# Two expert blocks in every fourth step to the end of the loop, and the sixteen zero fills moved to the first slots of the drain

## The chip, the cores and the metric

The kernel runs on one core of one Trainium2 chip. The metric is the time of one execution of the whole program on the device, in microseconds (us); less is better. Besides TensorE (PE), VectorE (DVE), ScalarE (ACT) and GpSimd (POOL), the sync engine (SP) matters here: it computes nothing, and issues most of the transfers, one after the other.

## What is computed

The reference takes 6250 rows of 256 numbers and 100,000 edges sorted by target. It normalizes the rows, and adds to each row a graph convolution and a linear attention. Then each normalized row z is sent to its two best of 16 experts:

```python
gate_logits = x @ gate_w + gate_b
topk_vals, topk_idx = jax.lax.top_k(gate_logits, K)          # K = 2 of E = 16
topk_w = jax.nn.softmax(topk_vals, axis=-1)
h = jax.nn.relu(jnp.einsum('bsh,ehf->bsef', x, w1) + b1)
expert_out = jnp.einsum('bsef,efh->bseh', h, w2) + b2
moe = jnp.sum(topk_w[..., None] * sel, axis=2)               # sel: the two chosen experts' rows
y = x + moe                                                  # then a last normalization of y
```

The output is the sum of the stages, 6250 x 256.

## The kernel before, in words

Rows are handled in 49 tiles (t) of 128, edges in 782 chunks (c) of 128. After a preparation of some 240 us comes **the loop** of 101 steps, a table that `plan` works out when the program is built. Step g (0 to 97) handles 8 chunks of edges: POOL issues 8 indirect gathers into a ring of 24 places in SBUF (`gather`, L1108), DVE makes one-hot matrices (L1585, L1590), PE adds the chunks up in PSUM with two `quad`s of 4 chunks (L2069). In between the tiles that are complete go through graph layer, attention, gate and sorting: `E`, `A`, `B`, `Q1`, `Q2` of a step are the tiles whose parts it does. After a tile's B, DVE has the slot of each row with each of its experts, and three steps later POOL scatters the rows to the DRAM tensor `disp`, ordered by expert (`dispatch`, L1116).

**A block** (in the code an item, k from 0 to 117) is 128 rows of one expert. SP loads it transposed from `disp` into one of four buffers (`item_rows`, `flip_rows`, L620), when the block four before it has left its buffer. PE multiplies by the first weights (`item_one`, L2168 and L2171: 28 matmuls), ACT takes the positive part (L1312), DVE makes the low half of the hidden rows (`hidden_lo`, L1814), PE multiplies by the second weights (`item_two`, L2182 and L2187: 13 matmuls), ACT evicts (L1319) and stores to the DRAM tensor `ytok` (L1306). Which expert and which rows make a block is decided on the device, two blocks at a time, by `pick_pair` on DVE (L1766 to L1787), out of the rows that `dispatch` has placed; blocks 58 to 73 are a fixed round over all experts (`flush`), and so are the last sixteen, 102 to 117. `room` says how many blocks `plan` may put into a step: two where the step's number is in `DOUBLE` and the step has no E and no B, else one. The second block of a step stands on PE behind the step's second quad, and its `item_two` in the next step behind that step's first quad.

**The drain** is what follows the loop: the blocks that found no step (`TAILK`), one in each slot j. PE does `item_one` of the next block and then `item_two` of this one, in two pairs of PSUM banks. In the same slots runs the last stage for tiles 0 to 31, in pieces of two tiles. POOL gathers each row's two expert outputs (`final_pool`, L814), DVE sums and measures (`final_sum`, L823 to L835) and normalizes (`final_norm`, L843 to L854), and SP stores both tiles and loads `zpd` and `zd` for tiles six later (`f_store` and `f_load`, L795, L789, L790). There are 8 buffers of tiles. `early` spreads the 32 pieces of work (`EARLY`: 16 sums, 16 norms) evenly over the slots, from two steps ahead of slot 0 on. **After the drain** the tiles 32 to 48 are done in the same way. Their gathers wait until all blocks are stored.

The last sixteen blocks read 128 rows of each expert that may lie partly behind the last row placed. So each expert's 128 rows behind its end are set to zero first: `fill_ends` (L983 to L988), 16 DMAs of 128 KB issued by SP, each with the register of its place loaded ahead. `item_rows` of the blocks from 102 on waits until all have landed. The places (`endoff`) are written by DVE in `ends`, behind the last pick. `left` is the semaphore by which DVE tells that such tables are written.

The part of `plan` that takes a block's step from `room`:

```python
while last < len(steps) and len(steps[last].item) >= room(steps[last], last):
    last += 1
at[k] = last
if last < len(steps):
    steps[last].item.append(k)
```

Of the kernel before, what the change touches and what calls it, by code (L numbers as in the profile page):

```python
# [10 lines left out]
P = 128  # L11
# [7 lines left out]
EXP = 16  # L19
CAP = 6528  # L20
# [7 lines left out]
ND = KB + 2 * JB  # L28
# [51 lines left out]
A_STEP = 16  # L80
NH = 4
NEARLY = 8
DOUBLE = range(32, 81, 4)


def static(k):
# [18 lines left out]
def room(s, i):  # L105

    return 2 if i in DOUBLE and not s.E and s.B is None else 1

# [99 lines left out]
class Own:  # L208
# [5 lines left out]
    def then(self, ins):  # L214
        self.n += 1
        ins.then_inc(self.on.sems[self.name], 1)
        return self.n
# [5 lines left out]
def build(nc, A, out):  # L223
# [11 lines left out]
    def sb(name, shape, dt):  # L235
        return ctx.enter_context(nc.sbuf_tensor(name, shape, dt))

    def dram(name, shape, dt):
        return nc.dram_tensor(name, shape, dt, kind="Internal").ap()
# [6 lines left out]
    S = Sems()  # L246
# [56 lines left out]
    tailt = sb("tailt", [P, EXP], f32)  # L303
# [21 lines left out]
    endoff = sb("endoff", [1, EXP], i32)  # L325
# [51 lines left out]
    disp = dram("disp", [DROWS, 2 * ROW], f16)  # L377
# [228 lines left out]
    redo = [misc[:, tok0 + 256 * i:tok0 + 256 * i + 256] for i in range(4)]  # L606

    def settled(e):
        e.wait_ge(S["left"], 3)
        f = e.value_load(flag[0:1, 2:3], min_val=0, max_val=1)  # L610
        return f

# [9 lines left out]
    def spare_sp(e):  # L622
        f = settled(e)
        st = rawslot[:, 13, :]
        with e.If(f):
            spare_idle(e)
            for i in range(SPARE):
                e.wait_ge(S["spare_dve"], i * SDV + 9)
                x = e.value_load(imax[0:1, 0, 0:1], min_val=0, max_val=EXP - 1)
                a_ = e.value_load(ioff[0:1, 0, 0:1], min_val=0, max_val=EXP * CAP - P)  # L630
                flip_rows(e, a_, 0)
                e.wait_ge(S["iz0"], 16 * (len(range(0, NI, 4)) + i + 1))
                for h, n in enumerate(("w1p", "w2p")):
                    e.dma_start(st[:, h * 1024:h * 1024 + 1024],
                                A[n][bass.ds(x, 1), :, :].rearrange("a p c -> (a p) c")).then_inc(S["spare_sp"], 16)
                e.wait_ge(S["spare_act"], i * SAC + SAC)
                e.dma_start(ytok[bass.ds(a_, P), :], iy[0].bitcast(i32)).then_inc(S["spare_sp"], 16)
                e.wait_ge(S["spare_sp"], i * SLD + SLD)
            for u in range(FB):
                e.wait_ge(S[f"sto{u}"], stored(FE, u))  # L640
            for t in range(FE):
                e.dma_start(redo[2], zpd[t * P:t * P + P, :]).then_inc(S["spare_sp"], 16)
                e.dma_start(redo[3], zd[t * P:t * P + P, :]).then_inc(S["spare_sp"], 16)
                e.wait_ge(S["spare_dve"], SPARE * SDV + RDV * (t + 1))
                e.dma_start(out[t * P:t * P + P, :], redo[3]).then_inc(S["spare_sp"], 16)
                e.wait_ge(S["spare_sp"], SPARE * SLD + RLD * (t + 1))

    def spare_dve(e):
        f = settled(e)
        sm, st = isml[:, 0, :], rawslot[:, 13, :]  # L650
        h = ih[0]
# [215 lines left out]
    with ctx:  # L867
# [3 lines left out]
        def _(e):  # L871
# [90 lines left out]
            def item_rows(k):  # L962
                if k >= 4:
                    on.wait_ge("il1", k - 3)
                if KF <= k < KB:
                    dispatched(FLT)
                    on.wait_ge("left", 1)
                    e.reg_load([yreg], flushoff[0:1, k - KF:k - KF + 1])
                elif k < ND:
                    j = pair_of(k)  # L970
                    dispatched(SEEN[j])
                    on.wait_ge("wlo", 4 * EXP)
                    on.wait_ge("pick", j + 1)
                    e.reg_load([yreg], ioff[0:1, j % 4, k % 2:k % 2 + 1])
                else:
                    dispatched(NT - 1)
                    on.wait_ge("fill", 16 * (2 + EXP))
                    e.reg_load([yreg], tailoff[0:1, k - ND:k - ND + 1])
                flip_rows(e, e.snap(yreg, min_val=0, max_val=DROWS - P), k % 4)

            freg = e.alloc_register(name="fill")

            def fill_ends():  # L983
                on.wait_ge("left", 2)
                for x in range(EXP):
                    e.reg_load([freg], endoff[0:1, x:x + 1])  # L986
                    e.dma_start(disp[bass.ds(e.snap(freg, min_val=0, max_val=EXP * CAP - P), P), :],  # L987
                                A["zrows"][0:P, :]).then_inc(S["fill"], 16)  # L988

            def final_stores(j):  # L990
                for c, p in early(j):
                    if c == "norm":
                        for t in PIECES[p]:
                            f_store(e, on, t)
# [43 lines left out]
            for j, k in enumerate(TAILK):  # L1038
                while loaded < min(k + 5, NI):
                    item_rows(loaded)  # L1040
                    loaded += 1
                if k == ND - 5:
                    fill_ends()
                final_stores(j - 1)
            final_stores(len(TAILK) - 1)
            spare_sp(e)
# [94 lines left out]
        def _(e):  # L1141
# [186 lines left out]
            def weights(n):  # L1328
                x = WORDER[n]
                for u in range(4):  # L1330
                    on.wait_ge(f"ld_wt{u // 2}", 16 * (n + 1))
                    if n >= 14:
                        on.wait_ge("wlo", 4 * n)
                    elif n >= 7:
                        on.wait_ge("ctxs", min(NT, (2048 * (x + 1) - 1) // 258 + 1))
                    hi_o, _, raw = wparts(x, wstage(n), u)
                    e.activation(hi_o, raw, ACT.Copy, scale=16.0).then_inc(S["whi"], 1)
# [65 lines left out]
        def _(e):  # L1403
            on = Waits(e, S)
            own = Own(on, "own_dve")
            then = own.then
# [342 lines left out]
            hold = {}  # L1749
# [58 lines left out]
            def hidden_lo(k, j):  # L1808
                j = max(j, 0)
                bank_ = (H[:, :], agg[:, 512:1024])[j % 2]  # L1810
                on.wait_ge("irelu", k + 1)
                on.wait_ge("il2", k if j == 0 else k - 1)
                h = ih[j % 2]
                e.scalar_tensor_tensor(h[:, 512:1024], bank_, 0.0, h[:, 0:512], ALU.max, ALU.subtract).then_inc(S["ilo"], 1)  # L1814
# [13 lines left out]
            def finals(j):  # L1828
                for c, p in early(j):
                    (final_sum if c == "sum" else final_norm)(e, on, own, p)  # L1830
# [55 lines left out]
            def ends():  # L1886
                own.wait_ge(hold["head"])
                own.wait_ge(own.n)
                then(e.tensor_copy(endoff[:, :], tailt[0:1, :]))
                f_ = then(e.tensor_scalar(fullb[:, :], tailt[:, :], 128.0, None, ALU.subtract))  # L1890
                x = then(e.tensor_tensor(isml[:, 3, 0:16], tailt[:, :], head[:, :], ALU.subtract))
                own.wait_ge(x)
                x = then(e.tensor_reduce(join[0:1, 1:2], isml[0:1, 3, 0:16], AX.X, ALU.max))
                own.wait_ge(f_)
                e.tensor_tensor(tailoff[:, :], fullb[0:1, :], snap[0:1, :], ALU.max).then_inc(S["left"], 1)
                own.wait_ge(x)
                x = then(e.tensor_scalar(join[0:1, 1:2], join[0:1, 1:2], 128.0, None, ALU.is_gt))
                own.wait_ge(x)
                x = then(e.tensor_tensor(join[0:1, 1:2], join[0:1, 1:2], join[0:1, 2:3], ALU.max))
                own.wait_ge(x)  # L1900
                e.tensor_copy(flag[0:1, 2:3], join[0:1, 1:2]).then_inc(S["left"], 1)

            def late_picks(slot_):
                for j, t in LATE:
                    if late_at(j) == slot_:
                        pick_pair(j, t)
                        if j == JF - 1:
                            flush()
                        if j == JF + JB - 1:
                            ends()  # L1910

            on.wait_ge("seen", NT)
            for j, k in enumerate(TAILK):
                if j == 0:
                    late_picks(0)
                    hidden_lo(k, 0)
                if j + 1 < len(TAILK):
                    hidden_lo(TAILK[j + 1], j + 1)
                finals(j)
                if j:  # L1920
                    late_picks(j)
# [413 lines left out]
```

## Time and profile before

| | |
|---|---|
| median of 3 runs | 1520.53 us (1517.84 to 1522.57) |
| profiled execution | 1516.08 us, of which the span of the trace 1514.2 us |
| PE busy | 1137.3 us (75%) |
| DVE busy | 1030.5 us (68%) |
| POOL busy | 1040.8 us (69%) |
| ACT busy | 452.7 us (30%) |
| the loop's last gather is issued at | 1268.49 us |
| the drain's first block starts on PE at | 1313.41 us |
| the drain's last block starts its last group on PE at | 1449.99 us |

The span runs from the first to the last instruction of the trace; 1.9 us of the execution lie around it. An engine's busy time leaves out register loads, branches and the issuing of DMAs; "issue" in a row is time in which an engine waited for nothing that the profile shows. SP's queue is written SPq, and the time of a row there is what the instruction held SP, not what the transfer took. PE is pipelined, so that the ends of its rows overlap the next one's start; starts are the better measure.

### The profile page before, as it was taken

The page shows a single profiled execution, that of the slowest core. Times are in us where ns is not written, and L with a number is a line of the kernel's source. Part 1 is how long each engine was busy: PE and PEld are TensorE (multiplying, and loading weights), DVE is VectorE, ACT ScalarE, POOL GpSimd, SP SyncE. Part 2 cuts the span into 40 slices and gives each one's busy share as a digit, 9 for nine tenths or more (in the row PEclk, how much of TensorE's full clock was granted, in tenths as well). Part 3 has the DMA queues.
Part 4 walks back from the last instruction along what each step waited for, and adds up shares of the span by engine and source line. Part 5 has one row for each costly group of instructions (what it writes and reads, how often), then busy time and mean ns, then how long its engine had stood idle before and what let it go on. Part 6 is the DMA issues. An engine that isn't in the chain of part 4 may idle for free. (4 is left out here: it accounts for less than half of the span.)

```text
span 1514.2 us, 34216 instructions
## 1 busy us (share of the span) xinstructions
PE 1137.3 (75%) x10594; PEld 986.1 (65%) x10594; DVE 1030.5 (68%) x3731; ACT 452.7 (30%) x1286; POOL 1040.8 (69%) x1068
## 2 busy tenths in 40 slices
PE   2338999667768988888888987887978878596930
PEld 2327788556557877777777876776867767575820
DVE  7863666577787767676675767665666566694767
ACT  3763455222222322222222222232222223221310
POOL 3657777767757777777777777777777776442535
PEclk9999999887778999999998999999989899798975
DMA  8238777544456666556555555566555555587965
GB/s 258 75 101 268 243 252 251 183 129 141 155 156 162 162 160 160 160 149 167 159 155 157 154 161 158 148 170 164 147 154 155 149 151 151 145 207 189 251 182 168
DMA packets 214482, 257.79 MB, mean 170 GB/s; under 512 B 92690, under 2 KB 177382, under 8 KB 213994
## 3 DMA queue, kind: packets, MB, share of 16 engines
q0 software_dynamic: 47328, 128.21, 31.0%
q1 hardware_dynamic: 149978, 111.76, 25.6%
q10 hardware_dynamic: 16992, 15.47, 3.3%
q8 instruction: 102, 1.67, 0.5%
q14 instruction: 82, 0.67, 0.2%
HBM read 179.45 MB, written 64.86 MB: 161 GB/s over the span
## 5 line engine op out<-in xcount | busy, mean ns | idle before, releaser
L1108 POOL DMA_INDIRECT ring<-ytab,src x782 | 778.1, 995 | 259.3 <-issue 234.1
L2069 PE MATMUL agg<-ring,oh 128*128 128x256 f16 x2346 | 313.5, 287 | 104.4 <-DMA ring<-ytab,src 104.4
L2069 PEld LDWEIGHTS agg<-ring,oh 128*128 128x128 f16 x2346 | 260.5, 117 | 137.1 <-issue 117.8
L2171 PE MATMUL H<-misc,big 128*128 128x128 f16 x2448 | 203.6, 229 | 0.3
L2171 PEld LDWEIGHTS H<-misc,big 128*128 (+1 forms) x2448 | 172.1, 102 | 15.9 <-issue 2.0
L2187 PE MATMUL OB<-big,misc 128*128 (+1 forms) x1224 | 156.2, 279 | 0.0
L814 POOL DMA_INDIRECT ring<-ytok,slot x74 | 73.3, 991 | 92.5 <-DMA out<-ring 50.6
L1116 POOL DMA_INDIRECT disp<-misc,slot x98 | 103.8, 1059 | 47.6 <-issue 45.4
L2187 PEld LDWEIGHTS OB<-big,misc 128*128 128x128 f16 x1224 | 119.5, 100 | 16.9 <-issue 0.2
L1590 DVE TENSOR_TENSOR oh<-eq,whl 128x1024 f16<-128x1024 f16 x196 | 127.1, 690 | 3.4
L1814 DVE SCALAR_TENSOR_TENSOR misc<-H,misc 128x512 f16<-128x512 f32 x102 | 70.3, 689 | 59.3 <-ACT misc L1312 57.8
L2168 PE MATMUL H<-sel,bank 80*128 (+1 forms) x408 | 94.2, 231 | 9.7 <-issue 6.6
L1312 ACT ACTIVATE misc<-H 128x512 f16<-128x512 f32 x102 | 60.5, 593 | 104.1 <-PE H L2171 89.0
L1319 ACT ACTIVATE misc<-OB 128x256 f32<-128x256 f32 x102 | 39.1, 383 | 156.9 <-PE OB L2187 156.5
L1259 ACT ACTIVATE small<-small,eps 128x1 f32<-128x1 f32 x98 | 28.8, 294 | 163.6 <-DVE small L1639 157.9
L1266 ACT ACTIVATE misc<-QT 128x256 f32<-128x256 f32 x49 | 18.8, 385 | 162.5 <-PE QT L2095 162.5
L1585 DVE TENSOR_TENSOR eq<-iota,loc 128x1024 f16<-128x1024 f16 x98 | 65.9, 672 | 0.0
L1612 DVE SCALAR_TENSOR_TENSOR misc<-misc 128x256 f32<-128x256 f32 x49 | 20.9, 429 | 63.3 <-ACT misc L1231 63.3
L2116 PE MATMUL QT<-wpj,misc 128*128 128x256 f32 x196 | 59.0, 429 | 0.0
L1283 ACT ACTIVATE misc<-GB 128x256 f32<-128x256 f32 x49 | 18.6, 379 | 134.9 <-PE GB L2123 132.9
L2095 PE MATMUL QT<-misc,wq 128*128 128x128 f32 x392 | 54.5, 283 | 5.0 <-DVE misc L1685 4.7
L2123 PE MATMUL GB<-ident,misc 128*128 128x128 f32 x98 | 23.3, 325 | 45.4 <-DVE misc L1696 45.4
(282 smaller groups left out, 2365.9 us busy)
## 6 DMA issues: line engine op xcount, KB each, us to landing
ytok<-misc ACTq DMA_DIRECT2D x118, 128.0 KB
ring<-ytab,src POOLq DMA_INDIRECT x782
big<-in_w1p SPq DMA_DIRECT2D x15, 512.0 KB, 4.2
big<-in_w2p SPq DMA_DIRECT2D x15, 512.0 KB, 6.3
big<-in_x_pt SPq DMA_DIRECT2D x7, 896.0 KB, 12.1
ytab<-big SPq DMA_DIRECT2D x7, 896.0 KB, 4.1
selfr<-ytab SPq DMA_DIRECT2D x49, 128.0 KB
xtd<-misc SPq DMA_DIRECT2D x49, 128.0 KB, 6.0
```

What stands on the lines that cost most here:

```text
L814: e.indirect_dma_start(v[0:n, j, :].bitcast(i32), None, ytok, bass.IndirectOffsetOnAxis(ap=slot[0:n, t, j:j + 1], axis=0)).then_inc(S[f"in ...
L1108: e.indirect_dma_start(ring[:, (c % R) * 512:(c % R) * 512 + 512], None, ytab[0:NP, :], bass.IndirectOffsetOnAxis(ap=src[:, c:c + 1], axis ...
L1116: e.indirect_dma_start(disp, bass.IndirectOffsetOnAxis(ap=slot[:, t, j:j + 1], axis=0), zhl[t % 2], None).then_inc(S[f"sc{j}_{t % 2}"], 16)
L1312: e.activation(ih[max(j, 0) % 2][:, 0:512], bank_, ACT.Relu).then_inc(S["irelu"], 1)
L1585: return then(e.tensor_tensor(eq[:, :, :, :], iota_p, spots(loc[:, :], g), ALU.is_equal))
L1590: e.tensor_tensor(oh[:, g % 2, j], eq[:, :, :, :], spots(whl[:, j, :], g), ALU.mult).then_inc(S["oh"], 1)
L1814: e.scalar_tensor_tensor(h[:, 512:1024], bank_, 0.0, h[:, 0:512], ALU.max, ALU.subtract).then_inc(S["ilo"], 1)
L2069: m_ = e.matmul(o_, oh[:, g % 2, wp, (c % 8) // 4, :, c % 4], ring[:, a_ + 256 * yp:a_ + 256 * yp + 256], start=False, stop=True, skip_gro ...
L2116: m_ = e.matmul(QT[:, 256:512], eb[:, o_ * 128:o_ * 128 + 128], wpj[:, o_, :], start=False, stop=o_ == 1)
L2168: e.matmul(o_, bank[:, f * 128:f * 128 + 128], who, start=True, stop=False)
L2171: m_ = e.matmul(o_, ws(h * 1024 + wp * 512 + f * 128, 128), zp[:, h * 128:h * 128 + 128], start=False, stop=(h == 1 and q == 2))
L2187: m_ = e.matmul(O, hp[:, f * 128:f * 128 + 128], w_, start=False, stop=(f == 3 and q == 2))
```

## The change

`DOUBLE` reaches to step 98 instead of 80. The fills are issued in four groups of four, in the drain's slots 1, 3, 5 and 7, instead of all sixteen in slot 12, where block 97 was; each group has one load of four registers. The places are written at the start of the drain, which adds one to the counts of `left`.

```diff
-DOUBLE = range(32, 81, 4)
+DOUBLE = range(32, 99, 4)
...
     def settled(e):
-        e.wait_ge(S["left"], 3)
+        e.wait_ge(S["left"], 4)
...
-            freg = e.alloc_register(name="fill")
-
-            def fill_ends():
+            fregs = [e.alloc_register(name=f"fill{i}") for i in range(4)]
+
+            def fill_ends(q):
                 on.wait_ge("left", 2)
-                for x in range(EXP):
-                    e.reg_load([freg], endoff[0:1, x:x + 1])
-                    e.dma_start(disp[bass.ds(e.snap(freg, min_val=0, max_val=EXP * CAP - P), P), :],
+                e.reg_load(fregs, endoff[0:1, 4 * q:4 * q + 4])
+                for r in fregs:
+                    e.dma_start(disp[bass.ds(e.snap(r, min_val=0, max_val=EXP * CAP - P), P), :],
                                 A["zrows"][0:P, :]).then_inc(S["fill"], 16)
...
-                if k == ND - 5:
-                    fill_ends()
+                if j % 2 and j // 2 < 4:
+                    fill_ends(j // 2)
...
             def ends():
                 own.wait_ge(hold["head"])
                 own.wait_ge(own.n)
-                then(e.tensor_copy(endoff[:, :], tailt[0:1, :]))
...
             on.wait_ge("seen", NT)
+            own.wait_ge(hold["tail"])
+            e.tensor_copy(endoff[:, :], tailt[0:1, :]).then_inc(S["left"], 1)
             for j, k in enumerate(TAILK):
```

Worked out by `plan`, the steps 84, 88, 92 and 96 now have two blocks. The drain has 29 blocks (89 to 117) instead of 33 (85 to 117). Two picks that were made in the drain are made in the loop, which leaves three of the five, and the 32 pieces of the last stage lie closer.

DVE, the end of step 84. L1666 is the last of the step's attention sum, L1766 and L1768 begin the pick:

```order
 L1639 BN_AGGR small<-small 128x2
 L1666 SCALAR_TENSOR_TENSOR misc<-misc 128x256
+L1814 SCALAR_TENSOR_TENSOR misc<-H,misc 128x512
 L1766 TENSOR_TENSOR isml<-seen_tail,head 128x16
 L1768 MAX isml<-isml 128x8
```

The step's second block adds its low half there; the same stands at the end of steps 88, 92 and 96.

SP before, in slot 12, behind the load of block 101. The three rows of a fill stand sixteen times:

```order
L974 TENSOR_LOAD ioff [waits k_pick,k_il1]
L979 ISA
L620 DMA_TRANSPOSE misc<-disp 128x4x128
...
L620 DMA_TRANSPOSE misc<-disp 128x4x128
L986 TENSOR_LOAD endoff [waits k_left]
L987 ISA
L987 DMA disp<-in_zrows 16x4096
L986 TENSOR_LOAD endoff
...
L978 TENSOR_LOAD tailoff [waits k_fill,k_il1]
L979 ISA
L620 DMA_TRANSPOSE misc<-disp 128x4x128
```

SP now, in slot 3, between the load of block 96 and that of block 97:

```order
L620 DMA_TRANSPOSE misc<-disp 128x4x128
L985 TENSOR_LOAD endoff
L987 ISA
L987 DMA disp<-in_zrows 16x4096
L987 ISA
L987 DMA disp<-in_zrows 16x4096
L987 ISA
L987 DMA disp<-in_zrows 16x4096
L987 ISA
L987 DMA disp<-in_zrows 16x4096
L974 TENSOR_LOAD ioff [waits k_il1]
```

Between two loads of blocks stand four fills and one register load, where sixteen fills and sixteen register loads stood.

## Rows read from the trace of the kernel before

**Rows 1.** Windows of stages: stretch, us, busy per engine (count), clock, DMA share, GB/s

```profile
0.00:1270.00 1270.00, 990.18 (x8993) 861.75 (x8994) 862.39 (x3129) 399.31 (x1136) 935.91 (x963) 0.92 0.58 167
...
1310.00:1452.00 142.00, 121.11 (x1370) 102.20 (x1370) 105.18 (x372) 38.77 (x101) 53.23 (x55) 0.93 0.84 208
1452.00:1514.20 62.20, 0.00 (x0) 0.00 (x0) 40.16 (x129) 4.50 (x18) 34.50 (x34) 0.53 0.55 165
...
1390.00:1450.00 60.00, 53.14 (x658) 49.03 (x659) 44.41 (x128) 18.22 (x48) 23.63 (x24) 0.91 0.96 237
```

**Rows 2.** Windows of two stretches of the loop, columns as above

```profile
500.00:600.00 100.00, 86.59 (x837) 75.78 (x837) 71.93 (x286) 26.90 (x81) 76.64 (x77) 0.97 0.65 167
1100.00:1200.00 100.00, 76.11 (x698) 68.08 (x696) 62.38 (x230) 23.54 (x72) 76.56 (x77) 0.90 0.58 155
```

**Rows 3.** Waits of POOL, 500 to 1100 us: us in total, times, longest

```profile
POOL ring L1108 <- PE agg L2069: 0.6, 2, 0.3
```

**Rows 4.** The longest wait of PE, 1100 to 1270 us

```profile
PE agg L2069 <- DMA ring<-ytab,src: 35.9, 12, 5.1
```

**Rows 5.** Timeline of PE, loop's end: start, us, line; in brackets the idle before

```profile
1264.96 1.47 PE L2187 MATMUL OB<-big,misc 128*128 x12
1269.08 1.50 PE L2069 MATMUL agg<-ring,oh 128*128 128x256 f16 x12 [2.65 <-DMA ring<-ytab,src]
```

**Rows 6.** Timeline of PE, the drain

```profile
1327.47 1.48 PE L2187 MATMUL OB<-big,misc 128*128 x12
...
1374.63 1.48 PE L2187 MATMUL OB<-big,misc 128*128 x12
...
1391.09 0.29 PE L2168 MATMUL agg<-sel,bank 80*128 80x128 bf16 x1 [11.05 <-DMA misc<-disp]
...
1405.82 1.47 PE L2187 MATMUL agg<-big,misc 128*128 128x256 f16 x12
...
1411.82 1.47 PE L2187 MATMUL agg<-big,misc 128*128 128x256 f16 x12
...
1422.36 0.29 PE L2168 MATMUL agg<-sel,bank 80*128 80x128 bf16 x1 [2.83 <-DMA misc<-disp]
...
1449.99 1.48 PE L2187 MATMUL OB<-big,misc 128*128 128x256 f16 x12
```

**Rows 7.** Timeline of SP's queue, the drain

```profile
1368.77 17.20 SPq L987 DMA_DIRECT2D disp<-in_zrows  x16
1388.33 1.26 SPq L620 DMA_TRANSPOSE misc<-disp  x1
...
1401.70 3.27 SPq L620 DMA_TRANSPOSE misc<-disp  x2
...
1423.56 2.88 SPq L620 DMA_TRANSPOSE misc<-disp  x2
...
1429.96 3.51 SPq L620 DMA_TRANSPOSE misc<-disp  x2
...
1437.37 2.88 SPq L620 DMA_TRANSPOSE misc<-disp  x2
```

**Rows 8.** Two lines of SP: duration of one in ns, min/median/max

```profile
L986 SPq TENSOR_LOAD <-endoff x16: 260/266/416, 1368.3 to 1385.0; - x16
L987 SPq DMA_DIRECT2D disp<-in_zrows x16: 517/517/1396, 1368.8 to 1385.5; - x16
```

**Rows 9.** The chain of waits at PE's second stop

```profile
1416.33 5.99 DMA misc<-disp
```

**Rows 10.** Waits of PE, 800 to 930 us, all of them

```profile
PE agg L2069 <- DMA ring<-ytab,src: 8.5, 4, 3.7
PE GB L2123 <- DVE misc L1696: 4.5, 4, 1.3
PE OB L2182 <- DVE misc L1814: 2.5, 2, 1.2
PE H L2168 <- issue: 1.9, 5, 0.6
```

## The prediction

> **What bounds the kernel now.** I read the windows first, since the program has stages. The loop's gathers end near 1270 us, 40 us follow in which the last tiles pass through, the drain fills 1310 to 1452, and 62.2 us of POOL gathers and DVE work close the span [rows 1]. Then I asked in each stage which wait ends last.
>
> In the loop it is POOL. It issues 77 indirect transfers per 100 us, both in the stretch where steps with two blocks occur (500 to 600) and where they have stopped (1100 to 1200), while PE is 86.59 us busy in the first and 76.11 in the second [rows 2]. The rest of those 100 us, 23.4, is 0.3 us behind each transfer. For a place in the ring, which only PE can free, it waited 0.6 us in 600 [rows 3]. PE is the one that waits: from 1100 to 1270 it stood 35.9 us for gathered chunks [rows 4].
>
> In the drain PE is bound while it is fed. From 1327.47 to 1374.63 it does 12 blocks, 3.93 us each. The blocks with a fixed expert take 3.00 us (1405.82 to 1411.82, two blocks). In between it stands for 11.05 us, waiting for the transposed load of block 102, and once more for 2.83 us at 1422.36 [rows 6]. SP's queue shows why: sixteen fills hold it for 17.20 us from 1368.77, and the next block load leaves only at 1388.33 [rows 7].
>
> **The change, part by part.** Durations come from the profiled execution, 1516.08 us.
>
> Loop. Each of four steps gets a block more, 3.93 us of PE at the drain's price, 15.7 us together. Per four steps (36 POOL transfers at 100/77 us, 46.8 us) PE has 35.9 x 46.8 / 170 = 9.9 us of waiting for chunks. So 3.9 us fit in, and POOL's pace stays: 0 us. Without that cover the price would be 15.7 us. DVE gets one row of `hidden_lo` more in each such step and is 62.38% busy there [rows 2]; SP's transposed loads come with it, in a stretch where the DMA engines' share is 0.58 [rows 2]. Both at 0. At the very end the cover is thinner. Step 96's second block puts its second group behind step 97's first quad, where a chunk wait of 2.65 us ended at 1269.08; that group is 1.47 us long at 1264.96 [rows 5] and stood ahead of the wait before. What follows in steps 97 to 100 moves by it, with its bias matmul, by **+1.6**. Bounds: 0 (the later waits of that chain swallow it) and +3.9 (a whole block).
>
> Drain, blocks with a picked expert. Thirteen instead of 17, at 3.93 us: **-15.7**. DVE also loses two picks from it. I cost that at 0, since PE sets the pace there.
>
> Fills. The stop of 11.05 us goes: **-11.05**. It needs all sixteen landed before block 102 is loaded, and in the new order the last group is issued in slot 7, block 102's load in slot 9. What do they cost where they stand now? A register load is 0.27 us and a fill 0.52 [rows 8]. With some 0.14 us of gaps behind each fill, as in the old pitch of about 1 us, a group is 0.27 + 4 x 0.66 = 2.9 us of SP. A pair of slots on SP (two transposed loads, two stores, four loads) takes 6.40 us at the best (1423.56 to 1429.96) [rows 7]. With a group that is 9.3 against 7.86 of PE, so SP falls behind by 1.4 us in each of four pairs, 5.8 us in all. SP may run three blocks ahead, 11.8 us, less what a load needs until PE has it: 2.8 us (issued 1388.33, PE starts 1391.09) to 6.0 (the chain's 5.99) [rows 6, 7, 9]. That leaves 5.8 to 9.0, just enough. I take **+1**, with bounds of 0 and 11.6 (all four groups exposed).
>
> The DMA engines carry the 2 MB of fills earlier, beside loads and stores. The rows say that this stretch has a share of 0.84 on average [rows 1]. The Trainium skill (DMA: Bandwidth & Descriptors, section "Issuing engines are not separate DMA queues") says that DMAs run on the same 16 engines whichever engine issues them, and interleave. By it, moving or regrouping an issue saves sequencer time alone and no transfer, and where those engines are full the sum would be the first rival's, a gain of 20 to 25 us instead of 28.
>
> Drain, last sixteen blocks. Here PE was not the bound before: from 1391.09 to 1449.99 + 1.48 they took 60.4 us [rows 6], where 16 x 3.00 + 1.6 (the second group of block 101) = 49.6 would do. Once the stops are gone SP is late next. From 1401.70 to 1437.37 it made five pairs in 35.7 us, 7.13 each [rows 7], against PE's 6.0 per pair. Eight pairs make 57.0. SP now arrives with part of its lead intact, of which I count 2 us. So 57.0 - 2 + 1.6 = 56.6, a gain of **-3.8**. Bounds: -10.8 (PE's own pace) and 0 (nothing, should the lead be used up by the fills).
>
> After the drain: the 62.2 us start when the last block is stored, and do the same work. 0.
>
> Sum: 1.6 - 15.7 - 11.05 + 1 - 3.8 = **-27.95**, so 1488.1 us for a profiled execution. The median of the runs stands 4.45 above the profiled one (1520.53 against 1516.08), which gives **1492.5**.
>
> **The rivals.**
>
> *The DMA engines set the drain.* It moved 208 GB/s x 142 us = 29.5 MB at a share of 0.84 [rows 1]. Four blocks go to the loop with 128 KB in and 128 KB out each, 1.05 MB. The remaining 28.5 MB at full share (208 / 0.84 = 248 GB/s) take 115 us, and at the 237 GB/s of 1390 to 1450 [rows 1] 120. The drain's window then shrinks by 22 to 27 us, with 1.6 us at the loop's end a gain of 20.4 to 25.4, or about 1497.5. For it: the share is 0.96 over the last blocks already [rows 1]. Against: part of that is the work that the fills had held back, and my own sum puts the drain's end at 1422 to 1424, within 3 us of this case's better end.
>
> *The fills stop PE.* If SP has no lead in slots 1 to 7 (loads landing after 6 us or more), the groups are exposed with 11.6 us instead of 1, and the last blocks gain nothing: -27.95 + 10.6 + 3.8 = -13.5, or 1507. Against it stands the lead worked out above, for it that the lead is used up to within a microsecond.
>
> *Slower: the block loads reach the loop before their rows.* Picks and uses stand closer now. The pair of blocks 84 and 85 was picked in step 94 and used from step 100 on; now it is picked in 92 and used in 96 and 97. Its load leaves SP a step earlier, and waits for a scatter that POOL issues after the gathers of group 94. Behind that load wait SP's loads and stores for the tiles. Should each of the pairs 84/85, 86/87 and 88/89 cost a step of 11.7 us, 35.1 us, the change loses: 1492.5 + 35.1 = 1527.6. It decides from 28 / 3 = 9.3 us per pair. Against it: between 800 and 930 us blocks are used three steps after their pick with two blocks in every fourth step, and PE's list of waits has no transposed load in it [rows 10].
>
> *The step's table does nothing.* Not so here: the four steps have neither E nor B, and the added rows of DVE show the blocks. Only the loop's own cover could fail: if PE's waits for chunks were not slack but a clock that the gathers keep, +15.7 would eat the drain's -15.7, leaving -12.3, or 1508. The even 77 transfers speak against it.
>
> **How the numbers follow.** Forecast 0.55; DMA-bound drain 0.22; exposed fills 0.10; loop without cover 0.03; late loads 0.04, of which 0.03 end slower and 0.01 in the middle; 0.06 for a smaller loss of several kinds, two thirds of it still faster. About 0.3% (4.6 us) is what a measurement can tell from no change. Faster 0.94, same 0.03, slower 0.03. The forecast's bounds give 1520.5 - 37.5 = 1483 at the low end (no loop end, no fill cost, PE's own pace) and -11.3, or 1509, at the high end (3.9 at the loop's end, fills exposed, no gain in the last blocks). The range of 1482 to 1506 holds the forecast, the DMA case and part of the third.
>
> **What would show it.** In the changed trace: POOL still at 77 transfers per 100 us up to 1270 us and its last gather of edges within 2 us of 1268.5; PE's waits for chunks between 1100 and 1270 down from 35.9 to about 20 us; the drain's first block near 1315; no PE wait over 3 us near its middle; SP's queue with four groups of four fills of some 2.9 us; PE's last group near 1422 to 1424; some 62 us behind it. I am wrong if POOL waits for PE's ring places, if the last blocks come every 3.0 us (more gain), or if PE waits for transposed loads between slots 3 and 12 (less).

## The result, and the profile after

The changed kernel takes **1498.82 us** (median of four runs, 1496.45 to 1502.07) where the kernel before took 1520.62 beside it (four runs): a ratio of 0.9859, with a 95% interval of 0.9834 to 0.9885. The gain is 21.8 us where 28 were forecast. The profiled execution took 1496.45 us, 19.6 less than the one before, and its span is 1494.5 us.

The windows of the changed kernel (stretch, us, busy per engine with counts, granted clock, DMA share, GB/s):

```profile
0.00:1270.00 1270.00, 1005.59 (x9173) 870.86 (x9174) 868.73 (x3150) 402.08 (x1144) 927.86 (x964) 0.93 0.60 168
1310.00:1432.00 122.00, 106.04 (x1211) 91.26 (x1211) 97.17 (x335) 35.28 (x94) 53.04 (x54) 0.94 0.90 231
1432.00:1494.50 62.50, 0.00 (x0) 0.00 (x0) 39.98 (x129) 4.50 (x18) 34.81 (x34) 0.51 0.56 167
1320.00:1370.00 50.00, 45.06 (x467) 35.48 (x468) 38.12 (x135) 13.96 (x36) 19.20 (x20) 0.97 0.85 215
1370.00:1420.00 50.00, 44.11 (x564) 41.38 (x561) 41.17 (x122) 14.85 (x41) 28.31 (x29) 0.93 1.02 263
1100.00:1200.00 100.00, 83.04 (x802) 74.36 (x803) 65.95 (x248) 25.80 (x78) 76.24 (x79) 0.93 0.60 163
```

Against [rows 1], PE does 15.4 us more in the same 1270 us of loop, and the drain's window is 20 us shorter. Against [rows 2], PE rose by 7 us in 1100 to 1200 and POOL did not slow down (79 transfers against 77). The use of the loop's cover is seen in PE's longest wait from 1100 to 1270 us, which was 35.9 us for chunks [rows 4]:

```profile
PE agg L2070 <- DMA ring<-ytab,src: 17.4, 10, 3.7
```

The waits of PE in the changed drain, 1310 to 1440 us. `H`, `agg` and `OB` are PSUM tiles, `misc<-disp` is a block's transposed load, L1814 is `hidden_lo`; total, times, longest:

```profile
PE agg L2169 <- DMA misc<-disp: 4.3, 3, 2.9
PE OB L2183 <- DVE misc L1814: 3.1, 3, 1.4
PE agg L2183 <- DVE misc L1814: 3.0, 1, 3.0
PE H L2169 <- DMA misc<-disp: 2.3, 1, 2.3
```

The stop of 11.05 us in [rows 6] is gone, and four shorter ones stand between 1358 and 1395 us: 1.16, 2.30, 2.88 and 2.96. The timeline of PE shows the two largest and what they leave behind (start, us, line; in brackets the idle before):

```profile
1374.52 1.47 PE L2188 MATMUL agg<-big,misc 128*128 128x256 f16 x12
1378.87 0.29 PE L2169 MATMUL agg<-sel,bank 80*128 80x128 bf16 x1 [2.88 <-DMA misc<-disp]
1378.95 0.84 PE L2172 MATMUL agg<-misc,big 128*128 128x128 f16 x6
...
1383.28 0.50 PE L2172 MATMUL H<-misc,big 128*128 128x128 f16 x6
...
1394.15 0.28 PE L2183 MATMUL agg<-bank,sel 80*128 80x256 bf16 x1 [2.96 <-DVE misc L1814]
...
1398.89 1.47 PE L2188 MATMUL OB<-big,misc 128*128 128x256 f16 x12
1401.89 1.47 PE L2188 MATMUL agg<-big,misc 128*128 128x256 f16 x12
...
1422.89 1.47 PE L2188 MATMUL OB<-big,misc 128*128 128x256 f16 x12
```

Behind the stop of 2.88 us six matmuls of the first group take 0.84 us instead of 0.50, four times over, so it also costs about 1.4 us of slower matmuls; behind the one of 2.96 it is 1.6 us (4.62 from 1394.27 to 1398.89 instead of 3.00). Behind the one of 1.16 us nothing slows down. The windows of the changed kernel just behind the first stop and a little later show the granted clock:

```profile
1379.00:1382.00 3.00, 3.00 (x30) 2.99 (x29) 2.85 (x9) 0.00 (x0) 1.24 (x2) 0.54 1.06 339
1383.00:1390.00 7.00, 6.95 (x96) 6.45 (x94) 5.14 (x16) 2.83 (x9) 5.00 (x5) 1.00 1.09 244
```

From 1398.89 on the blocks come every 3.00 us: the last ten run at PE's own pace, 30.02 us (30.48 and 32.64 in two more profiles of this program, below). Everything that the last sixteen lose, they lose before that: 27.37 us from 1371.52 (the second group of block 101) to 1398.89 for six blocks that need 18.0.

The timeline of SP's queue in the changed kernel shows the first and the last of the four fill groups, and transposed loads behind them:

```profile
1322.49 4.12 SPq L987 DMA_DIRECT2D disp<-in_zrows  x4
...
1356.67 2.73 SPq L987 DMA_DIRECT2D disp<-in_zrows  x4
1359.86 1.24 SPq L620 DMA_TRANSPOSE misc<-disp  x1
...
1365.74 2.95 SPq L620 DMA_TRANSPOSE misc<-disp  x2
...
1399.27 3.20 SPq L620 DMA_TRANSPOSE misc<-disp  x2
...
1406.17 2.87 SPq L620 DMA_TRANSPOSE misc<-disp  x2
...
1420.85 1.21 SPq L620 DMA_TRANSPOSE misc<-disp  x1
```

SP's pairs stay near the 7.13 us of the prediction: the eight from 1365.74 to 1420.85 take 6.9 on average (1399.27 to 1406.17 is 6.90). I counted the transposed loads back from the last one and set each beside the second group of its block. The load issued at 1320.74 is 19.6 us ahead of it (1340.35). Four groups later the one of 1359.86 is 11.7 us ahead (1371.52), and the next, of 1365.74, 8.8 us (1374.52). SP's lead of two blocks is what the fills used up.

The chain of waits in the changed kernel holds the second stop. PE waited for DVE's `hidden_lo`, and DVE, which works in order, stood at a tile whose load SP had issued at 1385.48:

```profile
1385.48 5.84 DMA ring<-zd
1391.34 0.48 DVE ring L823
...
1393.41 0.69 DVE misc L1814
1394.15 0.28 PE agg L2183
```

The account by marks, in us of the profiled executions (before, then after). The second group of the drain's first block: 1319.94, 1321.00, so +1.06. From there to that of block 101: 74.31 for sixteen blocks, 50.52 for twelve, so -23.79. The last sixteen: 55.74, 57.39, so +1.65. What follows the last group: 64.21, 65.59, so +1.4. The sum is -19.7, and the spans differ by 19.7.

### The profile page after: what moved, and what is told of

It reads as the page before. It is cut to its first block, busy times and chain, and to the rows that moved or that the text cites. A ratio compares the mean times of both kernels' runs of the same rounds, so it can differ in the third digit from the quotient of the medians.

```text
span 1494.5 us, 34204 instructions
## 1 busy us (share of the span) xinstructions
PE 1137.5 (76%) x10594; PEld 983.5 (66%) x10594; DVE 1031.0 (69%) x3731; ACT 451.5 (30%) x1286; POOL 1032.1 (69%) x1068
## 3 DMA queue, kind: packets, MB, share of 16 engines
q8 instruction: 101, 1.65, 0.4%
## 4 chain that ended last, share of the span: by engine, by line
POOL 35%; issue 12%; PE 11%; DVE 5%; DMA 4%; SPq 2%; ACT 1%; ACTq 0%; POOLq 0%; DVEq 0%
POOL ring L1108 29%; POOL disp L1116 4%; PE H L2172 3%; DMA ring<-ytab,src 2%; PE agg L2070 2%; POOL ring L814 2%; PE OB L2188 1%; PE agg L2172 1%; DVE misc L1814 1%; SPq L620 1%; PE agg L2188 1%; PE H L2169 1%; PE QT L2117 0%; SPq L795 0%; DMA oh<-ytok,slot 0%
## 5 line engine op out<-in xcount | busy, mean ns | idle before, releaser
L2172 PE MATMUL H<-misc,big 128*128 128x128 f16 x2496 | 208.0, 229 | 0.2
L1814 DVE SCALAR_TENSOR_TENSOR misc<-H,misc 128x512 f16<-128x512 f32 x104 | 71.6, 688 | 49.3 <-ACT misc L1312 49.3
L2169 PE MATMUL H<-sel,bank 80*128 (+1 forms) x416 | 95.8, 230 | 10.5 <-issue 7.5
L1612 DVE SCALAR_TENSOR_TENSOR misc<-misc 128x256 f32<-128x256 f32 x49 | 20.7, 426 | 61.6 <-ACT misc L1231 61.6
L1666 DVE SCALAR_TENSOR_TENSOR misc<-misc 128x256 f32<-128x256 f32 x49 | 20.2, 412 | 55.2 <-ACT misc L1268 55.2
L2169 PEld LDWEIGHTS H<-sel,bank 80*128 80x128 bf16 x416 | 42.6, 102 | 20.9 <-issue 20.3
## 6 DMA issues: line engine op xcount, KB each, us to landing
big<-in_x_pt SPq DMA_DIRECT2D x7, 896.0 KB, 12.8
```

The lines of the kernel that those rows point to most:

```text
L2169: e.matmul(o_, bank[:, f * 128:f * 128 + 128], who, start=True, stop=False)
L2172: m_ = e.matmul(o_, ws(h * 1024 + wp * 512 + f * 128, 128), zp[:, h * 128:h * 128 + 128], start=False, stop=(h == 1 and q == 2))
```

## Experiments

Kernels of one group below ran beside the same runs of the kernel before. "Drain" is the time from the second group of the first block to that of the last in the profiled execution: 130.05 us before (33 blocks), 107.91 in the changed kernel (29).

**Each half alone.** The kernel before with the new steps only:

```diff
-DOUBLE = range(32, 81, 4)
+DOUBLE = range(32, 99, 4)
```

> The table of steps of the change (29 blocks in the drain), the fills as before, all sixteen in the slot of block 97. Theory (additive parts): the loop part is worth its four blocks less the shift at the loop's end, 15.7 - 1.1 = about 14.5 us, so about 1506; the stop before block 102 stays, at 10 to 12 us. Rival (the drain is set by the DMA engines or by SP's queue, not by the number of blocks): the four blocks fewer are worth much less than 14 us alone, 1511 or more, since the pieces of the last stage only come closer together.

And the changed kernel with the old steps, so with the spread fills only:

```diff
-DOUBLE = range(32, 99, 4)
+DOUBLE = range(32, 81, 4)
```

> The fills in four groups in slots 1, 3, 5 and 7, the table of steps as before (33 blocks in the drain). Theory (additive): the stop of 11.05 us goes and a few us come back, gain 8 to 11 us, about 1511. With SP's queue full: the longer run of picked blocks lets SP catch up before the last sixteen, so that they take 55 us or less and the gain is over 11 us, 1508. Rival (the fills' time is only moved): gain under 5 us.

Loop only: 1507.1 us (1501.35 to 1510.49), ratio 0.9908 (0.9877 to 0.994), before 1520.59: -13.5. Fills only: 1506.82 (1503.25 to 1510.7), ratio 0.9921 (0.99 to 0.9942): -13.8. The forecast's terms were 1.6 - 15.7 = -14.1 and -11.05 + 1 - 3.8 = -13.85. Each half gives what its terms said. Together they give 21.8 instead of 27.3. The intervals reach 4.8, 3.2 and 3.9 us to either side, so these times alone don't show that the halves fail to add up.

The first kernel has its large stop still, the second has three small ones for transposed loads. Timelines of PE; first the loop-only kernel:

```profile
1383.02 0.29 PE L2168 MATMUL agg<-sel,bank 80*128 80x128 bf16 x1 [12.27 <-DMA misc<-disp]
```

then the fills-only kernel:

```profile
1370.90 0.23 PE L2169 MATMUL H<-sel,bank 80*128 x1 [2.31 <-DMA misc<-disp]
...
1401.20 0.23 PE L2169 MATMUL agg<-sel,bank 80*128 80x128 bf16 x1 [0.56 <-DMA misc<-disp]
...
1422.35 0.23 PE L2169 MATMUL agg<-sel,bank 80*128 80x128 bf16 x1 [2.96 <-DMA misc<-disp]
```

In the fills-only kernel the last sixteen took 52.71 us (1384.16 to 1436.87) against 55.74 before, a gain of 3.0 where 3.8 were forecast, and its expectation had said 55 us or less. In the changed kernel they took 57.39. So the halves meet in that one stretch. In the fills-only kernel seventeen picked blocks come first and nine of them lie behind the last fill; in the changed kernel thirteen come first and five lie behind. A picked pair gives SP 7.86 us for some 7.1 of work, which is where a lead is won back. That this is why the last sixteen differ was my reading of the two timelines, and no run moved the fills to other slots of the changed kernel to test it. The kernels with SP relieved, below, speak against it as the whole cause: a second thing differs too, the closer pieces of the last stage, which keep DVE busier in the changed kernel.

**The fills off SP.** The four groups stay in their slots, but ACT issues them (`fill_ends` itself moves to ACT's program as well):

```diff
-                if j % 2 and j // 2 < 4:
-                    fill_ends(j // 2)
                 final_stores(j - 1)
...
                 final_roots(j)
+                if j % 2 and j // 2 < 4:
+                    fill_ends(j // 2)
                 item_out(k, j)
```

> The change, with the four groups of fills issued by ACT's queue instead of SP's, in the same slots; the transfers and their bytes are the same. If SP's issue time is what the drain is short of (SP theory), the waits of PE for transposed loads near block 99 to 103 (1.16, 2.30, 0.23 and 2.88 us) go and the time falls by 3 to 6 us to about 1494. If the DMA engines are (DMA theory), nothing changes by over 1.5 us: 1497 to 1500.

1492.14 us (1490.28 to 1493.19), ratio 0.9818 (0.9802 to 0.9835): 6.7 less than the changed kernel, with the same transfers, where the SP theory had said 3 to 6. The two intervals touch, but all twelve runs of the changed program (see the repeats below) lie above these four. The drain is 102.42 us. Its windows and the waits of PE that name a transposed load:

```profile
1320.00:1370.00 50.00, 48.68 (x534) 38.76 (x535) 40.72 (x142) 14.03 (x37) 23.87 (x24) 1.00 0.97 246
1370.00:1420.00 50.00, 43.55 (x579) 39.74 (x577) 42.49 (x126) 16.13 (x44) 23.53 (x24) 1.00 1.08 265
```

```profile
PE H L2169 <- DMA misc<-disp: 1.5, 2, 1.3
```

PE waits 1.5 us for them instead of 6.6, keeps a granted clock of 1.00 where it had 0.97 and 0.93, and the DMA engines, called full by the rival, move 246 GB/s where they moved 215. SP now waits for others far more. For DVE to finish tiles it stood 5.1 us between 1310 and 1440 us in the changed kernel, and in this one:

```profile
SPq L795 <- DVE ring L854: 12.5, 11, 3.4
```

PE in turn has its larger waits for DVE now (1310 to 1445 us):

```profile
PE agg L2183 <- DVE misc L1814: 5.1, 6, 1.8
PE OB L2183 <- DVE misc L1814: 3.1, 3, 1.2
```

**The tiles' loads off SP.** The two loads of tiles 8 to 37 are issued by ACT instead, the fills stay on SP:

```diff
-        if t >= 2 and t + FB - 2 < NT:
+        if t >= FE and t + FB - 2 < NT:
             f_load(e, on, t + FB - 2)
...
                         final_root(e, on, p)
+                        if p >= 1:
+                            for t in PIECES[p]:
+                                f_load(e, on, t + FB - 2)
```

> The change, with the loads of zpd and zd for tiles 8 to 37 issued by ACT's queue behind the roots of their piece instead of by SP behind the stores; bytes the same, SP has 1.8 us less per pair of slots, ACT as much more. SP theory: the last sixteen blocks go from 57.4 us (3.6 each) towards PE's 3.0 each, and the time falls by 4 to 8 us, 1491 to 1495. DMA theory: the pace of the last sixteen stays at 3.5 us or more each, and the time within 2 us of 1498.8.

1497.76 us (1492.76 to 1502.75), ratio 0.9864 (0.9837 to 0.9891): no difference from the changed kernel, where the SP theory wanted 1491 to 1495, and the drain is 107.85 us. SP was relieved of more here than by the fills. The cost came back on ACT, whose queue also holds the relu that the next block needs; waits of DVE:

```profile
DVE misc L1817 <- ACT misc L1312: 20.3, 12, 4.0
```

In the changed kernel that wait is 6.7 us. ACT is no free place for issues either.

**Fewer bytes.** The loads of tiles 8 to 31 bring 64 of 256 columns, 4.7 MB less, with as many issues on SP. The kernel leaves out the rest of these tiles' sums, so its output is incomplete and only its time counts:

```diff
-        e.dma_start(v[0:n, 2, :], zpd[t * P:t * P + n, :]).then_inc(S[f"zin{t % FB}"], 16)
-        e.dma_start(v[0:n, 3, :], zd[t * P:t * P + n, :]).then_inc(S[f"zin{t % FB}"], 16)
+        m = 64 if FB <= t < FE else 256
+        e.dma_start(v[0:n, 2, 0:m], zpd[t * P:t * P + n, 0:m]).then_inc(S[f"zin{t % FB}"], 16)
+        e.dma_start(v[0:n, 3, 0:m], zd[t * P:t * P + n, 0:m]).then_inc(S[f"zin{t % FB}"], 16)
```

> The change, but the loads of zpd and zd for tiles 8 to 31 bring 64 of the 256 columns: 24 x 2 x 96 KB = 4.7 MB less, with the same instructions on every queue. (The sum of these tiles is therefore left incomplete.) DMA theory: 4.7 MB at 250 GB/s are 19 us of the drain; PE's and SP's own pace stop it at 3.0 to 3.3 us a block, so 8 to 15 us faster, 1484 to 1491. SP theory: SP's instructions are as many, and the pace of the last sixteen stays near 3.5 us; within 3 us of 1498.8.

1500.49 us (1499.72 to 1505.97), ratio 0.986 (0.981 to 0.9911): nothing gained. Windows of this kernel:

```profile
1320.00:1370.00 50.00, 46.23 (x495) 36.44 (x494) 39.14 (x148) 13.32 (x33) 18.14 (x19) 0.98 0.73 185
1370.00:1420.00 50.00, 43.86 (x556) 39.17 (x553) 40.72 (x121) 16.40 (x44) 29.77 (x31) 0.97 0.85 206
```

The DMA share fell from 0.85 to 0.73 and from 1.02 to 0.85, PE's busy time stayed within 1.2 us, and PE still waited 7.4 us for transposed loads (three of agg, 1.9, and three of H, 5.5). The rival of DMA-bound engines is out for this kernel: at 248 GB/s these 4.7 MB would be 19 us.

**Both.** Fills on ACT and the short loads, with the output incomplete as above:

> Fills on ACT's queue and the short loads together. DMA theory: as with the short loads alone or at most 3 us better, 1482 to 1488. SP theory: near the fills on ACT alone, 1490 to 1493. If each is a limit of its own, the two gains add: 1492 - 8 = 1484 or below. (The sum of tiles 8 to 31 is left incomplete.)

1489.98 us (1486.17 to 1492.31), ratio 0.9785 (0.9738 to 0.9831), drain 97.98 us. The interval overlaps that of the fills on ACT alone (0.9802 to 0.9835), 0.0033 or 5 us apart at the middle. Whether bytes count once SP is relieved isn't settled by it.

**More blocks in the loop.** Fills on ACT, and from step 82 on two blocks in every second step, so that 25 blocks are left for the drain:

```diff
-DOUBLE = range(32, 99, 4)
+DOUBLE = list(range(32, 81, 4)) + list(range(82, 99, 2))
```

> Fills on ACT's queue, and two blocks in every second step from 82 to 96: the drain has 25 blocks instead of 29. In the loop PE had 17.4 us of waits for chunks left between 1100 and 1270, four blocks are 15.7, so the loop stays at POOL's pace, +0 to +3. If the number of blocks set the drain, 4 x 3.9 = 15.7 us would come off; since by the DMA theory only the blocks' own bytes do (1.05 MB, 4.2 us), 1486 to 1490. No gain or a loss (1492 or more) if the loop's end moves by more than that.

1513.54 us (1503.45 to 1517.05, ten runs), ratio 0.993 (0.9904 to 0.9956): 21 us worse than the fills on ACT by the medians, 17 by the ratios, where 1486 to 1490 was expected. PE has no cover left and SP stops. First PE's wait for chunks from 1100 to 1270, 17.4 us in the changed kernel, then the wait of SP in the drain:

```profile
PE agg L2070 <- DMA ring<-ytab,src: 4.5, 4, 1.6
```

```profile
SPq L205 <- DMA disp<-in_zrows: 14.2, 1, 14.2
```

POOL keeps its 77 transfers per 100 us, but the first quad of step 97 begins at 1276.80 instead of 1265.44, the last tile's `GB` matmul (line 2124) at 1320.71 instead of 1306.26, and block 102 now wants its rows before the last fills, so its load stops SP for 14.2 us. The order of fills and blocks was not repaired for this, so the run doesn't price the dense steps alone.

**More fills.** Fills on ACT, and behind each group four more transfers of 128 KB, 2 MB in all, to a table that nothing reads; block 102's load waits for all 32:

```diff
+                for i in range(4):
+                    e.dma_start(dump[(4 * q + i) * P:(4 * q + i + 1) * P, :], A["zrows"][0:P, :]).then_inc(S["fill"], 16)
```

> Fills on ACT's queue, and beside each a second transfer of the same 128 KB to a tensor that nobody reads, 2.1 MB more of write traffic and as much read, issued by ACT, which had slack. DMA theory: the drain's time grows with its bytes, 2.1 MB at 250 GB/s = 8.4 us, so 1498 to 1501. SP theory: SP's queue is the same; ACT's extra 10 us of issue are spread over eight slots, within 2.5 us of 1492.1.

1504.98 us (1504.44 to 1509.26), ratio 0.9887 (0.9838 to 0.9936): 12.8 us more than with the fills on ACT alone by the medians, 10.5 by the ratios, and above what either theory had said. The waits of DVE say where; they are ACT's relu, held up in ACT's queue:

```profile
DVE misc L1817 <- ACT misc L1302: 17.9, 7, 4.8
```

ACT's issues and the bytes were doubled together, so this run doesn't tell them apart.

**Half as many issues, same bytes.** The loads of two tiles go out as one DMA each for `zpd` and `zd`, on SP:

```diff
+        for k, d in ((2, zpd), (3, zd)):
+            if m == 2:
+                i_ = e.dma_start(v[:, :, k, :], d[t * P:t * P + 2 * P, :].rearrange("(t p) c -> p t c", t=2))
...
-        if t >= 2 and t + FB - 2 < NT:
-            f_load(e, on, t + FB - 2)
+        if t >= 3 and t % 2 and t + FB - 3 < NT:
+            f_load(e, on, t + FB - 3)
```

> The change, with the loads of zpd and zd made for two tiles by one DMA each: SP issues two loads per piece instead of four, every byte and every descriptor as before, and nothing moves to another queue. SP theory: a pair of slots costs SP 0.9 to 1.0 us less (two loads of 0.36 and 0.45 us and their gaps), fifteen pairs in the drain make 14 us of SP, of which what was exposed comes off: 3 to 8 us faster than the change, 1491 to 1496. DMA theory: no difference beyond 2 us.

1494.1 us (1492.87 to 1496.91, five runs), ratio 0.9827 (0.9806 to 0.9847): 4.7 less than the changed kernel, with not a byte less, as the SP theory had said. The intervals overlap, but ten of the twelve runs of the changed program lie above all five of these. Timeline of SP's queue in it:

```profile
1392.01 3.29 SPq L620 DMA_TRANSPOSE misc<-disp  x2
1395.37 1.03 SPq L803 DMA_DIRECT2D out<-ring  x2
1396.63 0.38 SPq L795 DMA_DIRECT2D ring<-zpd  x1
1397.06 0.50 SPq L795 DMA_DIRECT2D ring<-zd  x1
1398.07 3.28 SPq L620 DMA_TRANSPOSE misc<-disp  x2
```

The pair shown is 6.06 us, near PE's 6.0. Where SP still lags it is for DVE, whose finished tiles it stores; from 1310 to 1440 us:

```profile
SPq L803 <- DVE ring L863: 14.6, 7, 5.2
```

The drain is 103.95 us.

**Both reliefs of SP.** Paired loads, and the fills on ACT:

> Paired loads on SP and the fills on ACT's queue. SP theory: SP has 26 us less of issue in the drain; what binds next is the low half of the hidden rows on DVE and ACT's queue, so the gain over the fills on ACT alone is smaller than that of the paired loads over the change: 1 to 4 us, 1488 to 1491. DMA theory: 1492 as with the fills on ACT alone.

1493.62 us (1491.98 to 1496.83, five runs), ratio 0.9817 (0.9796 to 0.9839): no better than either alone, where 1488 to 1491 was expected. In the profiled execution the drain is the shortest of all with full transfers, 100.06 us, but it begins at 1327.53 instead of 1321.00. One profile doesn't say whether that start belongs to the kernel. Over these profiles, the dense steps apart, it lies anywhere from 1317.55 to 1327.53.

**SP's time without transfers.** Two, then four register loads more on SP in each slot from 8 on:

```diff
+                if j >= 8:
+                    for _ in range(2):
+                        e.reg_load(fregs, endoff[0:1, 0:4])
```

> The changed kernel, with two more register loads on SP in each of the drain's last 25 slots (slots 8 to 32). No transfer is added, so the DMA engines carry the same bytes. One such load took 0.27 us. Theory (SP's own issue time paces the drain): 50 loads x 0.27 = 13.5 us more of SP; over slots 8 to 11 SP may still have some slack, so +8 to +14 us, 1507 to 1513, and the pairs of the last sixteen go from 7.1 to about 8.2 us. Rival (the bytes on the DMA engines set the pace and SP is only slow because its transfers are): nothing, 1498 to 1501, since 7.1 us per pair would absorb one more. Second rival (DVE or PE paces, SP only looks busy): nothing either.

> As before with four more register loads in each of the slots 8 to 32, 100 in all, 27 us of SP. Theory: +20 to +28 us, 1519 to 1527, pairs of about 9.3 us, twice the step of the run with two. Rivals: the first load hides in waits of SP, and only the second dose shows: less than +8 us with two loads and the rest with four, if SP has slack of about one microsecond a pair; 0 with both if SP doesn't pace at all.

1499.5 us (1497.84 to 1507.01), ratio 0.986 (0.9821 to 0.9898), and 1501.31 (1495.98 to 1507.11), ratio 0.9868 (0.9834 to 0.9901). By the letter the theory falls here. But the trace has no added load; only the fills' own four are left. Nothing reads the added values, which may be why. The second kernel's register loads on SP:

```profile
L985 SPq TENSOR_LOAD <-endoff x4: 301/306/317, 1323.7 to 1357.2; - x4
```

Both are the changed kernel once more. They test nothing of the theory and serve as repeats: three profiles of one program with drains of 107.91, 109.13 and 105.84 us and ratios of 0.9859 to 0.9868. So whether it is SP's own time that costs, or the queue of transfers that SP feeds, stays open; both fit the runs above.

**The drains side by side.** I split each profiled drain at the second group of block 101. The picked blocks before it are twelve in a drain of 29 blocks and sixteen in one of 33 (before and loop only with the large stop among them); the stretch behind it holds the last sixteen. For that stretch the table gives what PE waited for transposed loads and for DVE's `hidden_lo`, and how long DVE was busy, with its instructions, all in us:

| kernel | blocks | picked | last sixteen | PE for loads | PE for DVE | DVE busy |
|---|---|---|---|---|---|---|
| before | 33 | 74.31 | 55.74 | 5.2 | 0.5 | 44.41 (128) |
| fills only | 33 | 66.61 | 52.71 | 3.5 | 0.6 | 45.16 (130) |
| loop only | 29 | 59.79 | 54.53 | 0.3 | 5.6 | 46.87 (137) |
| changed | 29 | 50.52 | 57.39 | 2.9 | 4.2 | 47.54 (139) |
| changed, first repeat | 29 | 51.04 | 58.09 | 1.5 | 6.6 | 47.52 (138) |
| changed, second repeat | 29 | 50.14 | 55.70 | 1.0 | 5.5 | 47.48 (139) |
| fills on ACT | 29 | 46.77 | 55.65 | 1.5 | 6.1 | 47.61 (140) |
| paired loads | 29 | 46.49 | 57.46 | 4.0 | 3.9 | 48.53 (144) |
| paired loads, fills on ACT | 29 | 47.05 | 53.01 | 1.6 | 4.0 | 47.45 (139) |

The picked blocks tell a clear story. Twelve at 3.93 us are 47.2; with the fills on SP they take 50.1 to 51.0, with the short loads still 49.9, and in the three kernels at the foot of the table 46.5 to 47.1. So the fills' issues on SP cost 3 to 4 us there, and both single reliefs gained it back.

The last sixteen tell another. Relieving SP by one of the two didn't bring them clear of the 55.70 to 58.09 of the changed program. With 33 blocks PE waits there for loads; with 29 it waits more for DVE, but for the paired loads, where the two are level. The 32 pieces of the last stage lie closer in 29 slots, and DVE is busy for 47.5 us, where sixteen blocks at PE's 3.00 would give it 48.0. So DVE, which also stands for tiles' loads (6.4 us in the changed kernel's stretch), has nothing to spare at PE's pace. That DVE sets the pace there is a reading of the profiles: no run took work from DVE or spread the pieces otherwise, and most kernels have one profile.

## Why the prediction was right, and where it was off

- **Loop, 0 us for four blocks.** Right. POOL kept its pace, its last gather of edges began at 1264.38 (1268.49 before, so 4.1 us earlier, where within 2 us was said), and PE's waits for chunks fell from 35.9 to 17.4 where about 20 were said. The dense steps show the price without that cover.
- **Loop's end, +1.6.** The drain's first block came 1.06 us later, but that is luck in part: from the last gather to it lie 56.62 us instead of 51.45, 5.2 more and above the bound of 3.9, and the earlier gathers hid 4.1 of it. The repeats have 55.86 and 56.76. The fills-only kernel has 56.59 with the old steps, so the four blocks needn't be the cause; it stays open.
- **Four blocks less, -15.7, and the stop, -11.05.** Right in each half alone, within the noise: -13.5 and -13.8 against -14.1 and -13.85. In the account above they stand together, -23.79 for a forecast of 1 - 26.75 = -25.75.
- **Fills, +1.** A group took 2.73 to 4.12 us on SP, 2.9 forecast, but the cost was 3 to 4 us in this stretch. The pair of slots with a group was mis-sized: 9.3 us of SP by the forecast, 11.25 in the trace (the loads of blocks 94 and 102 leave at 1320.74 and 1365.74, four pairs apart). The lead fell from 19.6 to 11.7 us and PE began to stop for transposed loads at 1358.64, which the prediction had named as a sign of being wrong, with less gain.
- **Last sixteen, -3.8.** This step failed: "SP now arrives with part of its lead intact, of which I count 2 us". By the marks above they took 1.65 us more than before, 5.4 off. In the prediction's own terms, from block 102's first group to the end of the last, it is 60.6 us for a forecast of 56.6, against 60.4 before; the marks move the 1.4 us of slow matmuls behind the old stop to the blocks in front. The gain was nothing in all three profiles of the changed program (55.70 to 58.09 against 55.74). SP's lead is not the whole of it. DVE was left out of this sum, though its pieces come closer together: with the fills or half the loads' issues off SP the stretch still took 55.65 and 57.46, and PE's waits for `hidden_lo` in the changed kernel, 4.2 us, exceed its 2.9 for loads. The forecast treated the two halves as additive; alone the fills gave -3.0 here and the steps -1.2, both together +1.65 in one profile each.
- **After the drain, 0.** It came out at +1.4, for no reason that I can name (65.59 us, in the repeats 65.73 and 65.56, against 64.21).
- **The DMA-bound rival** named 1497.5 and was 1.3 us from the result, closer than the forecast, with a wrong mechanism. The Trainium skill (DMA: Bandwidth & Descriptors, "Issuing engines are not separate DMA queues") says that moving an issue saves sequencer time and no transfer. The runs agree that issues are what counted: moving sixteen of them, with the same transfers, gave 6.7 us, and 4.7 MB less gave none. A share of 1.02 beside it was no sign of a bound.
- The late loads and the loop without cover didn't happen. Of the rival at 1507 (exposed fills) half came true: the last blocks gained nothing, but the fills cost 3 to 4 us and not 11.6. 1498.82 lies within 1482 to 1506.

Faster than the changed kernel are the same with its fills on ACT, at 1492.14 us (ratio 0.9818), and, level with it, the ones with paired loads (0.9827) and with both (0.9817).

## What to carry to other kernels

Test two edits apart and together, and split their profiles at the same marks: the totals of the halves added up within the noise, and only the stretches showed where they met. When a change makes a stretch shorter, ask what else is spread over it: here the pieces of the last stage came closer, and an engine that had been costed at nothing, DVE, had no slack left. Read a queue's lead, from issue to use, slot by slot; it tells of the stop some blocks before it comes. After an engine has been relieved, look at who is waited for next. A high DMA share isn't a bound until fewer bytes give time back, and the cheap test is to shorten transfers at the same count, then to halve the count at the same bytes.

## What the hardware showed that I had not expected

- A stop of PE can cost more than its idle time: behind 2.88 us of waiting the granted clock was 0.54 from 1379 to 1382, so mostly its lower level of 1.2 GHz, and four rounds of six matmuls took 0.84 us each (0.77 the last) instead of 0.50. The length of the stop alone doesn't tell it: in the changed kernel one of 2.30 us at 1364.93 had rounds of 0.82 to 0.85 behind it, while one of 2.39 us at 1398.12 in the kernel before and one of 2.77 us at 1381.04 in the kernel with paired loads had 0.50.
- The DMA share can be read above 1: 1.02 at 263 GB/s in the changed kernel, 1.08 at 265 with the fills on ACT, for the same stretch. It doesn't tell how near the engines are to a limit: from 1370 to 1420 us, 263 GB/s in the changed kernel and 206 with the short loads went with 44.11 and 43.86 us of PE.
- One issue of a plain DMA of SP mostly takes 0.35 to 0.58 us, but single ones took 1.22 to 2.07 us in the drain, and a transposed load's issue 1.2 us or more. Two transposed loads and six plain ones took 6.5 to 7.4 us, which outlasts two slots of PE with 6.0.
